# A two-layer recurrent model on one core: first batch's x and some weights loaded through ScalarE's queue, and two orders changed in the turnover between batches

## What is computed

```
xn = layernorm(x)
s  = recurrent(xn)      # rms norm, delta = soft_clamp(softplus(xnr @ W_delta + b)),
                        # B, C = xnr @ W_B, xnr @ W_C, then a scan over time of 16 states a channel
g  = silu(shared + routed)
     shared = square(relu(xn @ Ws1)) @ Ws2
     logits = xn @ Wr; top 2; softmax; trunc; routed = the experts with a nonzero weight
x  = x + s * g
xn = layernorm(x)       # then projections q, k, v and the second router: second layer's inputs
s  = differential attention over 16 heads;  g = silu(experts with a capacity)
x  = x + s * g
```

## Time and profile before

| | |
|---|---|
| runs | 5478.05, 5480.47, 5493.4 us; median 5480.47 |
| the profiled execution's own time | 5481.77 us |
| its span, first to last instruction | 5480.0 us |
| mean granted clock of TensorE | 0.961 of full speed |
| TensorE busy (loads of weights apart) | 4872.8 us, 89% |
| VectorE busy | 4207.0 us, 77% |
| ScalarE busy | 3473.9 us, 63% |
| GpSimd busy | 1685.5 us, 31% |

### The profile page before, as it was taken

The page is one execution under the profiler, slowest core; times in us unless marked ns, Lnnn a source line. Parts: engine busy times, 40 slices in busy tenths (PEclk is TensorE's granted clock), DMA queues, the critical chain, the costliest instruction groups (busy, mean ns, idle before and its releaser), DMA issues. The chain is left out here.

```text
span 5480.0 us, 91530 instructions
## 1 busy us (share of the span) xinstructions
PE 4872.8 (89%) x32641; PEld 2260.3 (41%) x32641; DVE 4207.0 (77%) x4885; ACT 3473.9 (63%) x6262; POOL 1685.5 (31%) x1155
## 2 busy tenths in 40 slices
PE   5767767768774999998999999999999999999998
PEld 3224224225222888887333333333333333333335
DVE  5997996997996223222888888999999999999996
ACT  5765765665662111111777778888888888888883
POOL 1864873882883222222333331100001000010003
PEclk8998998998996999999999999999999999999999
DMA  3304403003004655553222223211122111221116
GB/s 96 122 8 145 139 0 128 11 1 107 17 0 137 204 192 188 188 200 127 59 68 68 68 68 88 51 42 34 34 50 57 37 34 34 54 55 35 34 34 183
DMA packets 354710, 437.91 MB, mean 80 GB/s; under 512 B 172347, under 2 KB 305302, under 8 KB 343382
## 3 DMA queue, kind: packets, MB, share of 16 engines
q1 hardware_dynamic: 311142, 222.98, 14.7%
q0 software_dynamic: 42784, 208.59, 11.4%
q10 hardware_dynamic: 320, 0.39, 0.0%
HBM read 287.44 MB, written 145.96 MB: 79 GB/s over the span
## 5 line engine op out<-in xcount | busy, mean ns | idle before, releaser
L1603 DVE TENSOR_REDUCE at_mpart<-at_ps 128x1 f32<-128x1024 f32 x2048 | 2412.8, 1220 | 338.7 <-PE at_ps L1496 302.7
L1588 ACT ACTIVATE at_E<-at_ps 128x512 f32<-128x512 f32 x4096 | 2126.5, 599 | 520.1 <-PE at_ps L1508 495.7
L1508 PE MATMUL at_ps<-at_qs,at_ks 98*128 98x512 bf16 x4096 | 1246.6, 386 | 49.3 <-ACT at_E L1588 39.0
L1516 PE MATMUL at_ps<-at_E,at_vst 128*32 128x256 f32 x16400 | 1101.4, 386 | 1.3 <-issue 1.3
L1508 PEld LDWEIGHTS at_ps<-at_qs,at_ks 98*128 98x128 bf16 x4096 | 315.3, 97 | 867.7 <-ACT at_E L1588 651.7
L1494 PE MATMUL at_ps<-at_ks,at_qs 64*128 64x512 bf16 x2048 | 634.8, 385 | 7.0 <-DVE at_mpart L1603 3.9
L1496 PE MATMUL at_ps<-at_kb,at_qb 64*128 64x512 bf16 x2048 | 634.9, 385 | 0.0
L857 POOL TENSOR_TENSOR l_work<-l_work 128x1024 f32<-128x1024 f32 x256 | 604.8, 2363 | 78.5 <-DVE l_work L866 70.4
L1516 PEld LDWEIGHTS at_ps<-at_E,at_vst 128*32 128x32 f32 x16400 | 428.9, 109 | 412.2 <-ACT at_E L1588 196.3
L753 PE MATMUL l_ps<-l_bc,l_sel 96*128 96x512 bf16 x1024 | 313.3, 395 | 277.3 <-DVE l_work L866 126.8
L1312 ACT ACTIVATE at_late<-at_ps 128x256 f32<-128x256 f32 x288 | 110.6, 384 | 639.4 <-PE at_ps L1255 635.3
(11 more groups left out here) (246 smaller groups left out, 4641.3 us busy)
## 6 DMA issues: line engine op xcount, KB each, us to landing
at_ks<-kp SPq DMA_DIRECT2D x396, 64.0 KB
xd<-l_zero SPq DMA_DIRECT2D x4, 5120.0 KB, 33.6
yd<-l_zero SPq DMA_DIRECT2D x4, 5120.0 KB, 33.5
at_qs<-qp SPq DMA_DIRECT2D x132, 128.0 KB
at_qb<-qp SPq DMA_DIRECT2D x132, 128.0 KB
qp<-l_work SPq DMA_DIRECT2D x32, 384.0 KB
kp<-l_work SPq DMA_DIRECT2D x32, 384.0 KB
ot<-at_osb SPq DMA_DIRECT2D x516, 17.0 KB
```

The lines of the kernel that those rows point to most:

```text
L1508: pe.matmul(S[chunk_bank(u, l)], m.ks[0:STACK + 2, j, bass.ts(kt, P)], m.qs[0:STACK + 2, j, half * QB + hf * BANK:half * QB + (hf + 1) * B ...
L1516: mm = pe.matmul(O[32 * q:32 * q + 32, :], m.vst[:, par, 2 * sl + kk, :], m.E[:, sl % 4, kk, bass.ts(q, QG)], start=(sl == 0 and kk == 0), ...
L1588: act.activation(m.E[:, sl % 4, c // 2, bass.ts(c % 2, BANK)], S[chunk_bank(u, l)], ACT.Exp, scale=SCALE).then_inc(s.ex, 1)
L1603: dve.tensor_reduce(m.mpart[:, job:job + 1], ring[n % 2].rearrange("p a b -> p (a b)"), AX_X, ALU.max).then_inc(s.ring_free, 1)
```

## The change

In the loading stage ScalarE's program starts four loads of x (into `x0T`, seen as natural tiles), then the six `wbc` pieces, `before` and `eid`; SyncE keeps the other 17. VectorE makes the statistics of x there, between its constants and its wait for the weights, and the first turnover starts with the square root. In the middle turnovers TensorE does the inner matmuls of the shared expert ahead of the router's, and VectorE clamps ahead of taking the top values. The first turnover keeps its order in both.

```diff
--- before.py
+++ after.py
@@ -64,7 +64,7 @@
 
     with ExitStack() as ctx:
         s = stage_sems(nc, ctx, f"turn{0 if nxt is None else nxt + 1}",
-                       "x_in0 x_in1 x_in2 x_in3 pstats pmv proot prstd pms prr x0 xr turned_r ev_r z zb t_abs t_exp t_ln sp th delta lnd sq u "
+                       "pstats pmv proot prstd pms prr x0 xr turned_r ev_r z zb t_abs t_exp t_ln sp th delta lnd sq u "
                        "bc bcx p1 r1 p2 r2 turned_x ev_x "
                        "sig silu turned_y g x1 stats mv root rstd xn stored turned_n ev_n "
                        "v v_out v_st0 v_st1 top idx lg chain counts base_ok gates gated kept "
@@ -85,7 +85,6 @@
         xflat = flat3(m.x)
         vs = xflat[:, 0:2 * 4 * VW].rearrange("p (j i c) -> p j i c", j=2, i=4)
         qr1 = xflat[:, 2 * 4 * VW:2 * 4 * VW + 2 * BANK].rearrange("p (j t) -> p j t", j=2)
-        x_in = (s.x_in0, s.x_in1, s.x_in2, s.x_in3)
         v_st, q_st = (s.v_st0, s.v_st1), (s.q_st0, s.q_st1, s.q_st2, s.q_st3)
         pm, psm = m.pmv, m.psmall
         mv, sm, t = m.mv, m.small, m.tsmall
@@ -99,10 +98,6 @@
             @block.sync
             def _(sp):
                 if first:
-                    for g in range(4):
-                        sp.dma_start(xp[:, bass.ts(g, 4), :], io.x[nxt:nxt + 1, bass.ts(g, BANK), :].rearrange("o (i p) d -> p (o i) d", p=P)).then_inc(x_in[g], 16)
-                    for g in range(4):
-                        sp.wait_ge(x_in[g], 16)
                     return
                 x1 = io.x1[done:done + 1, :, :].rearrange("o (i p) d -> p (o i) d", p=P)
                 for g in range(2):
@@ -217,13 +212,17 @@
                     pe.matmul(m.bank[0][:, 0:TILES * E1], m.before, chosen, start=True, stop=True)
                     pe.matmul(m.bank[1][:, 0:TILES * E1], m.ones, chosen, start=True, stop=True).then_inc(s.counts, 1)
 
-                def shared():
-                    pe.wait_ge(s.ev_x, 8)
+                def router():
                     for i in range(TILES):
                         for c in range(KD):
                             mm = pe.matmul(m.bank[4][:, bass.ts(i, E0)], m.x0T[:, c, bass.ts(i, P)], m.wr[:, c, :],
                                            start=(c == 0), stop=(c == KD - 1))
                     mm.then_inc(s.logit, 1)
+
+                def shared():
+                    pe.wait_ge(s.ev_x, 8)
+                    if first:
+                        router()
                     for g in range(4):
                         if g == 3:
                             pe.wait_ge(s.relu, 1)
@@ -231,6 +230,8 @@
                             mm = pe.matmul(m.bank[5 + g % 3], m.ws1[:, c, :], m.x0T[:, c, bass.ts(g, BANK)],
                                            start=(c == 0), stop=(c == KD - 1))
                         mm.then_inc(s.hid, 1)
+                    if not first:
+                        router()
                     for i in range(TILES):
                         pe.wait_ge(s.sqr, i // 4 + 1)
                         if i < 3:
@@ -295,19 +296,19 @@
                     dve.wait_ge(s.chain, n_chain[0])
 
                 def prep_stats():
-                    for i in range(TILES):
-                        if first:
-                            dve.wait_ge(x_in[i // 4], 16)
-                        dve.bn_stats(m.stats[:, i, :], xp[:, i, :]).then_inc(s.pstats, 1)
-                    for i in range(TILES):
-                        dve.wait_ge(s.pstats, i + 1)
-                        dve.bn_aggr(pm[:, i, :], m.stats[:, i, :]).then_inc(s.pmv, 1)
+                    if not first:
+                        for i in range(TILES):
+                            dve.bn_stats(m.stats[:, i, :], xp[:, i, :]).then_inc(s.pstats, 1)
+                        for i in range(TILES):
+                            dve.wait_ge(s.pstats, i + 1)
+                            dve.bn_aggr(pm[:, i, :], m.stats[:, i, :]).then_inc(s.pmv, 1)
                     dve.wait_ge(s.proot, 1)
                     dve.reciprocal(psm[:, 1, :], psm[:, 0, :]).then_inc(s.prstd, 1)
                     dve.wait_ge(s.prstd, 1)
                     dve.tensor_tensor(psm[:, 2, :], psm[:, 1, :], psm[:, 1, :], ALU.mult).then_inc(s.pms, 1)
                     dve.wait_ge(s.pms, 1)
-                    dve.wait_ge(s.pmv, TILES)
+                    if not first:
+                        dve.wait_ge(s.pmv, TILES)
                     dve.tensor_tensor(psm[:, 3, :], psm[:, 2, :], pm[:, :, 1], ALU.mult).then_inc(s.pms, 1)
 
                 def prep_norm():
@@ -517,8 +518,8 @@
                     split_low()
                     place_rows()
                     soft_plus()
+                    clamp()
                     shared_top()
-                    clamp()
                     shared_out()
                     inputs()
                     shared_prob()
@@ -535,7 +536,8 @@
                         act.activation(sig[:, bass.ts(g, 4), :], m.nat[:, bass.ts(g, 4), :], ACT.Sigmoid).then_inc(s.sig, 1)
 
                 def prep_roots():
-                    act.wait_ge(s.pmv, TILES)
+                    if not first:
+                        act.wait_ge(s.pmv, TILES)
                     act.activation(psm[:, 0, :], pm[:, :, 1], ACT.Sqrt, bias=m.eps[:, 0:1]).then_inc(s.proot, 1)
                     act.wait_ge(s.pms, 2)
                     act.activation(psm[:, 4, :], psm[:, 3, :], ACT.Sqrt, bias=m.eps[:, 1:2]).then_inc(s.proot, 1)
@@ -980,10 +982,22 @@
         sb("lg", [P, TILES, E0]); sb("top", [P, TILES, 8]); sb("prob", [P, TILES, E0])
         sb("eps", [P, 4]); sb("ones", [P, P]); sb("zero", [P, D]); sb("pmax", [P, 1]); sb("taken", [1, 1], I32)
         m = named(**t)
-        s = stage_sems(nc, ctx, "build_first_layer", "w_in zeroed")
-
+        s = stage_sems(nc, ctx, "build_first_layer", "w_in x_in0 x_in1 x_in2 x_in3 stats aggr")
+
+        x_in = (s.x_in0, s.x_in1, s.x_in2, s.x_in3)
+        x_first = m.x0T.rearrange("p k t -> p (k t)").rearrange("p (i d) -> p i d", d=D)
         with ExitStack() as c2:
             with nc.Block() as block:
+
+                @block.scalar
+                def _(act):
+                    for g in range(4):
+                        act.dma_start(x_first[:, bass.ts(g, 4), :], io.x[0:1, bass.ts(g, BANK), :].rearrange("o (i p) d -> p (o i) d", p=P)).then_inc(x_in[g], 16)
+                    for r in range(3):
+                        act.dma_start(m.wbc[:, :, 32 * r:32 * r + NS], io.W_B.rearrange("(c p) n -> p c n", p=P)).then_inc(s.w_in, 16)
+                        act.dma_start(m.wbc[:, :, 32 * r + NS:32 * r + 32], io.W_C.rearrange("(c p) n -> p c n", p=P)).then_inc(s.w_in, 16)
+                    act.dma_start(m.before, io.before).then_inc(s.w_in, 16)
+                    act.dma_start(m.eid, io.eid).then_inc(s.w_in, 16)
 
                 @block.sync
                 def _(sp):
@@ -993,16 +1007,13 @@
                             (m.wq, io.WqT.rearrange("(c p) n -> p c n", p=P)), (m.wk, io.WkT.rearrange("(c p) n -> p c n", p=P)),
                             (m.wvg[:, :, 0:D], io.WvT.rearrange("(c p) n -> p c n", p=P)),
                             (m.wvg[:, :, D:VW], io.WgT.rearrange("(c p) n -> p c n", p=P)),
-                            (m.bvg[:, 0:D], io.bv.partition_broadcast(P)), (m.before, io.before), (m.eid, io.eid)]
-                    for r in range(3):
-                        cols.append((m.wbc[:, :, 32 * r:32 * r + NS], io.W_B.rearrange("(c p) n -> p c n", p=P)))
-                        cols.append((m.wbc[:, :, 32 * r + NS:32 * r + 32], io.W_C.rearrange("(c p) n -> p c n", p=P)))
+                            (m.bvg[:, 0:D], io.bv.partition_broadcast(P))]
                     with nc.allow_non_contiguous_dma(reason="columns of 128 numbers"):
                         for t, v in ((m.nw, io.norm_weight), (m.bd, io.b_delta), (m.ds, io.D_skip), (m.bq, io.bq), (m.bk, io.bk)):
                             sp.dma_start(t, v.rearrange("(c p) -> p c", p=P)).then_inc(s.w_in, 16)
                         for t, v in cols:
                             sp.dma_start(t, v).then_inc(s.w_in, 16)
-                    sp.wait_ge(s.w_in, 16 * (5 + len(cols)))
+                    sp.wait_ge(s.w_in, 16 * 25)
 
                 @block.vector
                 def _(dve):
@@ -1013,6 +1024,12 @@
                     dve.memset(m.eps[:, 2:3], -CENTER / HALFSPAN)
                     dve.memset(m.bvg[:, D:VW], 0.0)
                     dve.memset(m.base, 0.0)
+                    for i in range(TILES):
+                        dve.wait_ge(x_in[i // 4], 16)
+                        dve.bn_stats(m.stats[:, i, :], x_first[:, i, :]).then_inc(s.stats, 1)
+                    for i in range(TILES):
+                        dve.wait_ge(s.stats, i + 1)
+                        dve.bn_aggr(m.pmv[:, i, :], m.stats[:, i, :]).then_inc(s.aggr, 1)
                     dve.wait_ge(s.w_in, 16 * 25)
                     for k in range(KD):
```

## The result

The changed kernel takes 5449.82 us (median of six runs, 5442.04 to 5461.24), the kernel before 5480.25 (six, 5478.05 to 5493.4): ratio 0.9938, interval 0.9924 to 0.9951, 30.4 us less. The profiled execution took 5452.1 us, its span is 5450.3 instead of 5480.0, and the mean granted clock 0.965 instead of 0.961.

What follows compares the result with a forecast made beforehand. Barriers put each stretch on the path: x bounds the head, the chain from router to inputs the middle turnovers. 6.0 + 3 x 8.3 = 30.9 us off 5481.8, and 1.3 less for the median, gave 5450; range 5438 to 5470.

Steps and rivals of the forecast that it cites:

- soft-plus late next: Middle turnovers: with inner matmuls first, tanh waits for VectorE's soft-plus and runs 461.6 to 465.7 us.
- Loads, 6.0 us: Loading stage: x travels beside the weights, transfers end at 18.6 us, square root starts at 22.7 instead of 28.65.
- It hardly overlaps: Rival, loading stage: x adds its whole 6.7 us of transfer, so the head gains 2.9 us; 5453, chance 0.12.
- a gain of 2.0 us: Loading stage: by the skill's rule on issuing engines, the head would gain just x's issue time, 2.0 us.
- Statistics, nothing: Loading stage: 5.85 + 1.15 us of statistics go under the weights' wait and cost nothing.
- Inner matmuls first: Middle turnovers: inner matmuls run at full clock, 448.59 to 455.6 us; ScalarE's last square ends at 456.9 instead of about 469.1.
- The half-clock rival: Middle turnovers: inner matmuls run at 1.2 GHz, projections 5.9 us later each; 5492, chance 0.05.
- Copies: Middle turnovers: clock returns near 470, sixteen copies end at 476.5 us instead of 484.8, a gain of 8.3 each.
- the gaps: Before the last copies of turnovers two and three: 3.8 us more than in the first, left in the sum.
- The ring behind: VectorE, ScalarE and stores from the projections on, while GpSimd's scatter runs until 503.6 us; no change in the sum.
- the stores absorb it: Rival, projections: the ring gains nothing while overlapping the scatter, the 24.9 us return and 5475 is left; chance 0.13.

Runs made afterwards that it cites:

- the one-queue run: Kernel before with early statistics and all 29 loads on SyncE's queue, x first, turnover orders as before: 5380.59 us, ratio 1.0004 to before.
- both orders: Kernel before with the new TensorE and VectorE orders in the middle turnovers, loads as before: 5367.95 us, ratio 0.9976 to before.
- the head alone: Changed kernel with both middle-turnover orders put back, so only the loads and early statistics are new: 5375.7 us, ratio 0.9995 to before.
- Without the scatter: Changed kernel with GpSimd's 32 indirect row writes left out in the middle turnovers: 5426.38 us, ratio 0.989 to the kernel before.
- the interleaved kernel: Changed kernel with VectorE's inputs and prob tiles spread between the pieces of its projections: 5489.54 us, ratio 1.0003 to the kernel before.

## Why the prediction was right, and where only its sum was

The number held: 5450 forecast, 5449.82 measured, inside the range and faster by more than 0.3%. The forecast's mechanism held too: x under the weights, dense matmuls at full clock, soft-plus late next. But that the number held to 0.2 us is luck. Its terms add up to 30.9 us, the changed stretches gave 19.6, and 10.0 that no term had came from elsewhere.

- **Loads, 6.0 us.** Measured 5.0 at the root and 4.5 at the flag. They started at 3 us, as taken. The work was 0.15 + 6.86 + 5.75 + 5.5 = 18.3 us of full share where 17.8 was worked out, and it was done at a mean share of 1.07 over the 17 us, where the sum let the highest share of before, 1.14, hold all along: that is the 1.4 us. VectorE followed the end of the transfers by 1.1 us instead of 1.5, so 1.0 is left at the root. "It hardly overlaps" (2.9) is excluded, and so is a gain of 2.0 us. The prediction took that 2.0 from the Trainium skill, "DMA: Bandwidth & Descriptors", section "Issuing engines are not separate DMA queues". The section is on which engine issues, and the head gains by when x is issued: the one-queue run has x first on SyncE's own queue and its root at 23.55.
- **Statistics, nothing.** Right: done 5.6 us before the last weight. The bare table load of 1.28 us came as forecast.
- **Inner matmuls first.** Relative to the counts, forecast and first middle turnover after: inner matmuls to 7.0 and 7.0; last square 8.3 and 8.3; tanh from 13.0 to 17.1 and from 13.0 to 17.2; router to 17.0 and 16.5; second clamp to 18.4 and 18.5; top values to 20.1 and 20.1. Soft-plus is late next, as said. The half-clock rival is excluded: 1.00 under the inner matmuls.
- **Copies.** This is the step that was off, in the first middle turnover. Forecast to end 27.9 us after the counts, measured 32.9. The clock returned 25.0 us after the counts instead of 21.4: the sum took over 4.1 us of dense work from rows 5 and 8, but the outer matmuls had been going for 8.6 us by then, with 1.36 us idle among them. This costs some 1.7 (3.6 us of copies at 0.85 instead of 0.44 each); the rest is gaps. The forecast left the gaps in for turnovers two and three only, where rows 9 have them, and took the first as free of them. Counts to projections is 38.8 and 41.0 in those two, around the 40.1 (48.4 - 8.3) of the forecast; in the first it is 41.3 instead of 36.3. So 3.3 + 9.6 + 7.4 = 20.3 us arrive at the projections instead of 24.9. On B and C, where no gaps are, it is 35.3 to 37.7 with both orders and 43.9 to 44.0 in the head alone and in before: the 36.3 of the forecast is what the mechanism gives by itself.
- **The ring behind** (the projections, up to the flag). The sum took it as unchanged; after takes 28.9, 30.5 and 28.6 us where before took 27.7, 27.6 and 27.4. That is 5.2 us given back, and leaves 15.1. Without the scatter on A it is 27, so the part of the rival "the stores absorb it" that lies in the scatter is borne out in a mild form. That stores do it is not shown: in the first ring ScalarE waits 6.9 us for stores after and 7.1 before.
- **Sum.** 4.5 + 15.1 = 19.6 from the changed stretches instead of 30.9. The attention's first 1024 exponentials and what follows gave 10.0 that no term of the sum had. In the experiments on A the same 1024 exponentials took from 739.7 us (the interleaved kernel) to 749.4 (the repeat of the changed one), so the changed kernel's own two executions differ by 5.2 us there; of before there is one trace on A. Whether the change has a part in it was not settled. For it speaks that the repeat gained 32.6 us again, against it that the time turned up in other stretches. On B, where the same exponentials take 681 to 688 us, the two parts gave 4.3 and 12.0 us, 0.3% in all.

What the change saves in its own stretches is thus 19.6 us on A, and on B 24.6 by its two parts: 4.6 up to the first flag (102.5 us in the head alone, 107.1 with the orders alone) and 20.0 in the turnovers. What arrives at the end is 16 us on B, less than that, as the scans between took 16.2 us more with both orders, at a lower clock, and 30 us on A, more than that, for a reason that stays open.

## What to carry to other kernels

Put dense work that feeds another engine ahead of tiny matmuls: here they take the clock down, and whoever waits behind them pays twice. Loads overlap a stage only as far as the transfers do: which engine issues them did not matter, but issuing what the next stage does not read one stage later, with the table load hidden beside it, took 7 us more off the head. Judge a change of 5 to 20 us in 5000 by its own stretches in the trace: here unchanged stretches moved by 7 us (a scan) to 12 us (the attention's start on A), so that a kernel that leaves work out measured 22 us slower.

## What the runs showed of the hardware

- The same program takes 5380 us on two chips and 5485 on the third. Some 70 us of the difference lie in the first 1024 exponentials of the attention (752.1 against 680.4 us), where TensorE idles 57 us on the slow one.
- On that chip VectorE starts copies 1.4 us apart or more (instead of some 0.44), with "remote" as the releaser, while GpSimd issues indirect DMAs; without them it does not. In one kernel ScalarE's pieces stand 7 to 8 us apart in the same way, until GpSimd is done. What holds them is not shown.
- Identical scans take 341 us at a mean granted clock of 0.95 or 348 at 0.93, and which of them it is changes from kernel to kernel where the edit lies outside the scans. Why it changes is open; no edit tested the clock by itself.
- An edit can do harm alone and good beside another: VectorE's order took 2.5 us more in the first middle turnover alone and gave 1.6 on the mean behind TensorE's new order.
